# First attention of a four-stage kernel: one tile form less, one preparation per step, reciprocals widened on GpSimd, residual bias a step later

## The reference

```python
def _L0_xattn_ref(x, y, wq, bq, wk, bk, wv, bv, wo, bo):      # x is layer-normalised
    q = (x @ wq + bq).reshape(B, Sq, H, D).transpose(0, 2, 1, 3)
    k = (y @ wk + bk).reshape(B, -1, H, D).transpose(0, 2, 1, 3)
    v = (y @ wv + bv).reshape(B, -1, H, D).transpose(0, 2, 1, 3)
    scores = jnp.einsum('bhqd,bhkd->bhqk', q, k) / jnp.sqrt(jnp.asarray(D, x.dtype))
    attn = jax.nn.softmax(scores, axis=-1)
    out = jnp.einsum('bhqk,bhkd->bhqd', attn, v)
    out = out.transpose(0, 2, 1, 3).reshape(B, Sq, E)
    return out @ wo + bo
...
x = x + jnp.tanh(g_xattn[0]) * _L0_xattn_ref(_layernorm(x, axis=-1), ctx_768, ...)
```

## Time and profile before

| | |
|---|---|
| median of 3 runs | 909.94 us |
| the profiled execution, its own time | 908.92 us |
| its span, first to last instruction | 907.1 us |
| PE busy, of the span | 777.2 us |
| DVE busy | 690.6 us |
| ACT busy | 568.8 us |
| POOL busy | 469.1 us |
| first attention | the first 320 us of the span |

### The profile page before, as it was taken

The page is one execution under the profiler, slowest core; times in us unless marked ns, Lnnn a source line. Parts: engine busy times, 40 slices in busy tenths (PEclk is TensorE's granted clock), DMA queues, the critical chain, the costliest instruction groups (busy, mean ns, idle before and its releaser), DMA issues. The chain is left out here.

```text
span 907.1 us, 26462 instructions
## 1 busy us (share of the span) xinstructions
PE 777.2 (86%) x8408; PEld 600.7 (66%) x8408; DVE 690.6 (76%) x2993; ACT 568.8 (63%) x1209; POOL 469.1 (52%) x505
## 2 busy tenths in 40 slices
PE   4999999999999889998998987876887888888870
PEld 2566666666666557676676665766787777788870
DVE  3989889888998968888887877455676565668764
ACT  3777777777777566878888775354354454455430
POOL 3554445444555012377777766645555555555560
PEclk9999999999999989999999999688899999999995
DMA  9101000010000020011111111311223322246638
GB/s 243 43 23 43 20 20 20 27 34 20 20 20 2 3 59 10 13 51 46 42 52 45 49 45 40 89 49 49 68 78 86 90 70 79 76 122 171 176 91 280
DMA packets 62329, 58.12 MB, mean 64 GB/s; under 512 B 10327, under 2 KB 52216, under 8 KB 62232
## 3 DMA queue, kind: packets, MB, share of 16 engines
q1 hardware_dynamic: 44664, 34.42, 14.3%
q0 software_dynamic: 8640, 17.84, 5.7%
q10 hardware_dynamic: 8928, 4.70, 1.8%
HBM read 32.91 MB, written 24.02 MB: 63 GB/s over the span
## 5 line engine op out<-in xcount | busy, mean ns | idle before, releaser
L1132 POOL DMA_INDIRECT contributions<-v_heads,d_token x142 | 137.9, 971 | 105.6 <-PE bc_bank L1882 67.9
L1863 PE MATMUL bc_bank<-d_xT,d_w 128*128 128x128 f32 x1136 | 161.6, 287 | 35.6 <-DVE d_xT L1381 30.1
L1863 PEld LDWEIGHTS bc_bank<-d_xT,d_w 128*128 128x128 f32 x1136 | 143.0, 197 | 46.1 <-DVE d_xT L1381 37.6
L1116 POOL DMA_INDIRECT sorted_rows<-r_send,r_slots x128 | 126.7, 990 | 47.3 <-issue 40.3
L1640 ACT ACTIVATE b_hidden<-bc_bank 128x256 f32<-128x256 f32 x142 | 54.5, 384 | 143.8 <-PE bc_bank L1863 126.5
L494 POOL TENSOR_SCALAR a_k_heads<-a_kT,first 128x512 f32<-128x512 f32 x60 | 93.1, 1569 | 0.8 <-ACT a_kT L547 0.8
L1634 ACT COPY d_w<-w 128x512 f32 x142 | 87.1, 614 | 4.2 <-issue 1.9
L412 DVE TENSOR_REDUCE a_neg_max<-a_scores 128x16 f32<-128x1024 f32 x64 | 78.1, 1221 | 8.1 <-PE a_scores L663 6.9
L571 ACT ACTIVATE a_probs<-a_scores 128x1024 f32<-128x1024 f32 x64 | 65.6, 1025 | 29.5 <-PE a_scores L673 29.4
L578 ACT COPY a_probsT<-a_probsT_bank 128x512 f32<-128x512 f32 x128 | 74.8, 584 | 13.4 <-PE a_probsT_bank L690 12.8
L690 PE MATMUL a_probsT_bank<-first,a_probs 128*128 128x128 f32 x512 | 79.7, 278 | 2.2 <-ACT a_probsT L578 0.3
(11 more groups left out here) (213 smaller groups left out, 1894.1 us busy)
## 6 DMA issues: line engine op xcount, KB each, us to landing
d_rows<-sorted_rows SPq DMA_DIRECT2D x142, 65.0 KB
X<-in_x SPq DMA_DIRECT2D x16, 256.0 KB, 3.1
b_hidden<-contributions SPq DMA_DIRECT2D x8, 512.0 KB
b_weighted<-contributions SPq DMA_DIRECT2D x8, 512.0 KB
out_x<-X ACTq DMA_DIRECT2D x16, 256.0 KB
ctxT<-in_ctx_T SPq DMA_DIRECT2D x16, 192.0 KB, 3.0
c_ctxT<-in_ctx_T SPq DMA_DIRECT2D x16, 192.0 KB
contributions<-v_heads,d_token POOLq DMA_INDIRECT x142
```

Source lines behind the costliest of these rows:

```text
L1116: pool.indirect_dma_start(dispatch.rows, bass.IndirectOffsetOnAxis(ap=slots[n % 2][:, k, j:j + 1], axis=0), send[n % 2][k][:, j, :], None) ...
L1132: pool.indirect_dma_start(dispatch.contributions, bass.IndirectOffsetOnAxis(ap=token[:, t % KEEP:t % KEEP + 1], axis=0), shares[t % KEEP], ...
L1863: last = pe.matmul(uv[m % 2][:, bass.ts(i, P)], w12[m % 3][:, bass.ts(i, P)], xT[m % 4][:], start=True, stop=True)
```

## The change

1. **Tile forms** (PE). KEYS, QUERIES and VALUES are computed in pieces of 32 columns instead of 64, so that their forms are 128*32 and 96*32, beside the 128*32 of L719. There are twice as many matmuls, four side by side instead of two. The subtraction of the maxima is split in two halves of 64 columns, form 32*64, as the scores.
2. **One preparation per step** (PE and ACT). KEYS moves from step 0, ahead of the output projection, to step 3 of the group before, after the probabilities times values.
3. **Reciprocals** widened by GpSimd, first in its step, for the tile whose widened reciprocals TensorE transposes in that same step (`widen`). VectorE no longer does it; `rec` gets a second buffer.
4. **GpSimd's other work**: `spread_k` is divided over steps 0, 1 and 2 (one, two and one heads). `add_bias` moves to the end of step 0 of the next group. `later_zeros` moves into step t = 62.

The diff, without what only renames:

```diff
-    rec = sb("a_rec", [P, H], F32)
+    rec = [sb(f"a_rec{i}", [P, H], F32) for i in range(2)]
...
-    PREP_AT = ((ROWS,), (QUERIES,), (VALUES,), ())
+    PREP_AT = ((ROWS,), (QUERIES,), (VALUES,), (KEYS,))
+    SPREAD_AT = ((0,), (1, 2), (3,), ())
...
+    def preparations(t, u, g0):
+        first = [(1, KEYS)] if static(t) and t == 0 else []
+        parts = first + [(2 if k == KEYS else 1, k) for k in PREP_AT[u % GT]]
+        return [(group_at(g0, more), (u // GT + more) % 2, k) for more, k in parts if group_at(g0, more) is not None]
...
 # VectorE, step
-                    if not static(m) or m >= 1:
-                        dve.wait_ge(wide_rec_ready, m)
-                    dve.reciprocal(rec[:], denom[:]).then_inc(rec_done, 1)
+                    if not static(m) or m >= 2:
+                        dve.wait_ge(wide_rec_ready, m - 1)
+                    dve.reciprocal(rec[u % 2][:], denom[:]).then_inc(rec_done, 1)
...
-                if m is not None:
-                    if not static(m) or m >= 2:
-                        dve.wait_ge(spread_mm, m - 1)
-                    dve.wait_ge(rec_done, m + 1)
-                    dve.tensor_copy(wide_rec[u % 2][:], rec[:].unsqueeze(2).broadcast_to([P, H, DH])).then_inc(wide_rec_ready, 1)
...
 # GpSimd
-            def spread_k(g, par):
-                wait_alone(pool, prep_ev, PREP * g + KEYS + 1)
-                if not static(g) or g >= 2:
-                    wait_alone(pool, scores_mm, GT * (g - 1))
-                for j in range(4):
+            def spread_k(g, par, heads):
+                if heads[0] == 0:
+                    wait_alone(pool, prep_ev, PREP * g + KEYS + 1)
+                    if not static(g) or g >= 2:
+                        wait_alone(pool, scores_mm, GT * (g - 1))
+                for j in heads:
                     last = pool.tensor_scalar(keys_of_head(par, j), kT[:],
                                               c.head_of_group[:, j:j + 1], None, ALU.mult)
-                last.then_inc(k_heads_ready, 1)
+                if heads[-1] == 3:
+                    last.then_inc(k_heads_ready, 1)
+            def widen(n, par):
+                wait_alone(pool, rec_done, n + 1)
+                if not static(n) or n >= 2:
+                    wait_alone(pool, spread_mm, n - 1)
+                pool.tensor_copy(wide_rec[par][:], rec[par][:].unsqueeze(2).broadcast_to([P, H, DH])).then_inc(wide_rec_ready, 1)
             def step(t, u, g0):
+                n = tile_now(t, 3)
+                if n is not None:
+                    widen(n, (u + 1) % 2)
+                if static(t) and t == TILES - 2:
+                    later_zeros(pool, c, dispatch)
                 if u % GT == 0:
                     g = group_at(g0, 2)
                     if g is not None:
                         deviation(g)
-                if u % GT == 1:
+                g = group_at(g0, 1)
+                if g is not None and SPREAD_AT[u % GT]:
+                    spread_k(g, (u // GT + 1) % 2, SPREAD_AT[u % GT])
+                if u % GT == 0 and not (static(t) and t < GT):
                     g = group_at(g0, 1)
-                    if g is not None:
-                        spread_k(g, (u // GT + 1) % 2)
-                    g = group_at(g0, 2)
                     if g is not None:
                         add_bias(g)
...
 # TensorE, prepare
-                        for odd in range(2):
-                            last = pe.matmul(prep[S * odd:S * odd + S, bass.ts(h, GW // 2)], w[:, bass.ts(h, D // 2)],
+                        for strip in range(4):
+                            odd, s = strip // 2, strip % 2
+                            last = pe.matmul(prep[bass.ts(strip, STRIP), bass.ts(h, GW // 2)], w[:, bass.ts(2 * h + s, STRIP)],
...
 # TensorE, step
-                        last = pe.matmul(scores[(u + 1) % 2][:, s, :], rows[bass.ts(s, STRIP), :], c.head_cols[bass.ts(s, STRIP), :],
-                                         start=False, stop=True, skip_group_check=True)
+                        for b in range(2):
+                            last = pe.matmul(scores[(u + 1) % 2][bass.ts(b, S), s, :], rows[bass.ts(s, STRIP), bass.ts(b, S)],
+                                             c.head_cols[bass.ts(s, STRIP), :], start=False, stop=True, skip_group_check=True)
...
-                if u % GT == 0 and g is not None:
-                    prepare(g, (u // GT + 1) % 2, KEYS)
...
-                    for k in PREP_AT[u % GT]:
-                        prepare(g, (u // GT + 1) % 2, k)
+                for g, par, k in preparations(t, u, g0):
+                    prepare(g, par, k)
```

More of the change, by code:

```diff
@@ L521, in _ @@
             loop_steps(pool, 2 * GT, TILES // (2 * GT) - 2, LAST, step)
-            later_zeros(pool, c, dispatch)
             c.ln.deviation(pool, 0)
@@ L579, in keep_transposed @@
                              probsT_bank[:]).then_inc(pT_ev, 1)
-                g = group_at(g0, 1)
-                if u % GT == 0 and g is not None:
-                    evacuate(g, (u // GT + 1) % 2, KEYS)
                 if tile_now(t, 2) is not None:
@@ L591, in step @@
                     act.copy(heads_raw[:], pv[:, 0]).then_inc(raw_ready, 1)
-                g = group_at(g0, 1)
-                if g is not None:
-                    for k in PREP_AT[u % GT]:
-                        evacuate(g, (u // GT + 1) % 2, k)
+                for g, par, k in preparations(t, u, g0):
+                    evacuate(g, par, k)
                 if tile_now(t, 2) is not None:
@@ L642, in prepare @@
                     for b in range(GB):
-                        for odd in range(2):
-                            last = pe.matmul(prep[S * odd:S * odd + S, bass.ts(b, D // 2)], ctxT[par][:, bass.ts(b, S)],
+                        for strip in range(4):
+                            odd, s = strip // 2, strip % 2
+                            last = pe.matmul(prep[bass.ts(strip, STRIP), bass.ts(b, D // 2)], ctxT[par][:, bass.ts(2 * b + s, STRIP)],
                                              c.wv0[:].rearrange("p (u h w) -> p h u w", h=2, w=DH)[:, odd],
```

## The result

The changed kernel takes 959.10 us, the median of 4 runs (957.95 to 963.11), against 909.54 (908.78 to 912.01): a ratio of 1.055, 95% interval 1.051 to 1.0585. The forecast was 959. The profiled execution took 959.77 us, 50.85 more than that of before.

A forecast was written before the change was run, and what follows sets the result against it. PE bounds the first attention. Gains from forms and KEYS against a wait on GpSimd's queue in 13 groups sum to +35.9 us; with +13 for the clock, 908.9 becomes 957.8, plus 1 for the median 959 us; range 937 to 983.

The forecast's parts named there:

- A line by columns through the bias: GpSimd's widening copy: estimated by columns between a 4-column record of 0.23 us and the bias of 1.27, taken as 0.46.
- so I take half: PE's clock after each of 13 stalls: half of 2.0 us lost, 1.0 per stall, +13 us in all.
- the row of 2.70 us at 1.00: Trace of the kernel before: an idle stretch of 2.70 us at 312.6 us that left the clock at 1.00.
- I count no gain of its own: VectorE relieved of the widening: worth nothing where PE bounds the step, and in step 3 KEYS covers it.
- The branch is paid as before: The loop's branch, where 0.48 us of issue stands ahead of the scores: its cost was taken as unchanged.
- The contention that the prediction weighed: GpSimd's copy holding VectorE's splitting of the maxima by up to 0.46 us: costed at nothing; +14, or 973, if uncovered.
- The subtraction's drain: Start of each of 64 steps on PE: one change of tile form fewer, worth 0.10 us per step.
- A net stall of 1.3 us: Step 1 in 13 groups: the net stall at which the gains of 1.13 us in 15 groups are used up.
- clock holds: Rival: PE stalls in step 1 but the clock does not fall; 946 us, chance 0.22.
- half a stall: Rival: the widening comes earlier than GpSimd's queue says, 2 us less per stall; 933 us, chance 0.08.
- faster: Rival: no stall in step 1, and 15 groups gain 1.13 us each; 892.5 us, chance 0.06.
- clock in full: Rival: the clock falls at each stall, 13 us more, 972 or so; chance 0.20, shared with uncovered contention.

The follow-up runs named there:

- e1: Changed kernel with GpSimd's widening at the head of the step before, for tile t-2 instead of t-3; ratio 0.978 to the kernel before.
- e10: The same kernel as e1 run again on another chip; ratio 0.9785 to the kernel before.
- e4: Changed kernel with 14 unused matmuls on PE ahead of its wait for the widened reciprocals; ratio 1.0332 to the kernel before.
- e3: Changed kernel with the bias moved from the end of step 0 to the end of step 2 on GpSimd; ratio 1.0284 to the kernel before.
- e2: Changed kernel with the widening back on VectorE, all other parts kept; ratio 0.9915 to the kernel before.
- e6: e1 with the subtraction of the maxima again in two matmuls of form 32*128; ratio 0.9789 to the kernel before.
- e5: e1 with KEYS, QUERIES and VALUES again in pieces of 64 columns; ratio 0.9828 to the kernel before.
- e7: e1 with KEYS back in step 0 ahead of the output projection; ratio 0.9876 to the kernel before.
- e9: Changed kernel with the bias and the head of the keys both out of GpSimd's step 0; ratio 0.9944 to the kernel before.

## Why the prediction was right, point by point

The time of 959 was met, and the mechanism is shown: e1 takes away the place in the queue and nothing else, and the loss turns into a gain. The sizes behind it were less good than the sum. (The three measured parts add up to the difference of the stretches by construction: e1 or e10 against before, e4 against e1 or e10, after against e4.)

| term | predicted | measured |
|---|---|---|
| forms, KEYS, VectorE's relief | -17.4 | -17.7 to -19.5 (e1, e10) |
| the queue, 13 stalls | 13 x 4.1 = +53.3 | +47.8 to +49.6 (e4 over e1, e10) |
| the clock | +13 (ends 0 and 26) | +20.4 (e4) |
| start-up | 0 | +2.6; it varies by up to 3.9 over all kernels |
| behind the first attention | 0 | -2.2 |

- **The chain on GpSimd was right link by link.** Counted from the start of step 1: the statistics end at 1.00 (predicted 1.00), the deviation at 2.57 (2.58), the head takes 1.54 (1.55), the bias 1.21 (1.27). The first wrong link is the copy, 0.29 instead of 0.46, with 0.06 for waits instead of 0.25. So the transpose starts at 5.66 instead of 6.10, and the stall is 3.66 instead of 4.1 beyond the 2.00 at which PE wants it. A line by columns through the bias was the wrong scale for it: the bias adds two operands, the copy reads one. Whether that is the reason no run shows.
- **The clock was mis-sized.** The step "so I take half" failed. The clock fell at every one of the 13 stalls of 3.5 us; the row of 2.70 us at 1.00 was no guide to that, since in e3 waits of 2.24 to 2.42 us made it fall in seven groups of 13. That is the rule of the Trainium skill ("TensorE: Matmul & The Clock Gate", HAM oscillation) as the prediction quoted it, and the trace agrees with it: 20.4 us stand nearer to the 26 of all 13 stalls than to 13. It is less than 26 because a fall costs 1.46 us in a group of the loop (22.31 - 20.85), not 2.0. The 2.0 was too much even by its own row: 4.00 us at 0.57 lose 4.00 x 0.43 = 1.7, and 13 x 1.7 = 22.
- **"I count no gain of its own" for VectorE was wrong.** With the other parts in place it is worth 9 to 11 us (e2 against e1 and e10), 3.4 to 4.9 of them up to step 1 of group 14 and some 6 in the one hold behind it. The statement was only looked at in step 3; but in step 1 the copy on VectorE was held by GpSimd, and what stood behind it met the bias.
- **"The branch is paid as before" was wrong.** It costs 0.54 us each time before (0.69 against 0.15) and at most 0.18 in e1 and e10: about 2 us that the sum did not have.
- **The contention that the prediction weighed**, a GpSimd copy that holds VectorE's splitting of the maxima, cost nothing that shows. The records of that line above 0.3 us are 14 of 64 before, 14 in e10 and 1 in after, none above 0.63, and in e10 PE is busy throughout. So the hold did not come in most steps, which the 973 of the prediction rested on.
- **The subtraction's drain was too large**, 6.4 against 1.3 to 3.1 (e6), and the drains of QUERIES and VALUES too small, 3.0, or 4.5 with KEYS counted too, against 5.9 to 7.7 (e5). The reading of 0.10 from the overlaps was right as a distance between two starts and wrong as a step's gain.
- **KEYS was right in the steps**: step 0 3.96 (3.88), step 3 4.33 (4.34). As a whole it is worth 8.1 to 9.9 us (e7) against 8.0, but part of that is the branch, so the agreement of the whole is in part luck.
- **Slips in the working.** A net stall of 1.3 us instead of 4.1 wants the widening 2.8 us earlier, at 155.2, and not 2.6 at 155.4. The two upper ends together are 986, above the 983 of the range. Neither mattered.

The sum of the gains came out because these errors offset one another, and the total because too long a stall met too cheap a clock: that the time was met to 0.1 us is luck. Where the clock holds, in e4, step 1 of the 13 groups lasts 7.99 to 8.16 us instead of 8.45.

The rivals: "clock holds", 946, fell with the row at 0.54; "half a stall", 933, and "faster", 892, with the 46.3 us of waits. For "clock in full", 972, only the price was too high. The first stage grew by 53.1 us where 48.9 were forecast: +7.4 from the clock and +2.6 from the start-up, about -4.6 from the stall and -1.2 from the gains.

## What to carry to other kernels

Before an instruction moves to an engine with time to spare, write down what stands ahead of it in that engine's queue and when the first of these can start. An engine that is idle half of the time (GpSimd works for 113.53 of 237 us) is still late for everything behind its one long wait; one step further up the same copy is free. And where several small parts each shorten another engine's step, try them together, and look where the difference lies before you call it an interplay: alone they gave 2.8 and 8.6 us here, together 17.7 to 19.5, and some 5 us of the difference were one hold behind the loop.

## What was unexpected of the hardware

- A copy on VectorE that else takes 0.22 us lasted 4.56 us while GpSimd went from one instruction to the next, a memset among them (e2).
- The clock: it fell to half at each idle time of 3.5 us, during it or up to about 1 us behind it, and stayed there for some 3.5 us, behind the first two for over 6. It fell in seven groups of 13 at idle times of 2.24 to 2.42 us, never at 0.7 to 0.9, and never where PE did matmuls that nobody reads (after, e3, e9, e4).
- The loop's branch costs PE 0.54 us a time in the kernel before and 0.13 in e10, where KEYS stands ahead of it and VectorE is early.
- Twice as many matmuls of half the columns cost nothing: KEYS in 16 records of 32 columns takes 1.05 us, in 8 of 64 columns 1.08.
- The same kernel takes 833 to 917 us on three chips, while the instructions of the first attention last the same in the runs on all of them.
